# An audio tower on one core: the router's exponential takes the negated maximum as a bias, and every engine's steps are reordered

## The chip, the cores and the metric

The kernel runs on one core of a Trainium2 chip. The metric is the device time of one execution in microseconds. Of the kernel before, three runs are shown: 429.63, 430.35 and 431.35, median 430.35.

The core has five instruction queues that work side by side and wait for each other through semaphores: TensorE (PE in the rows, its weight loads PEld), VectorE (DVE), ScalarE (ACT), GpSimd (POOL) and SyncE (SP), which here starts all DMA transfers.

## The reference

The input x holds 16 sequences of 375 rows of 128 numbers. Each goes through three stages, the last two added to their input:

```
z, f, o = tanh / sigmoid / sigmoid of a width-2 convolution of x     # 374 rows
c_t = f_t c_(t-1) + (1 - f_t) z_t;   h = o * c                       # recurrence
a  = layernorm(h)
q, k, v = a W_qkv + b;  scores over 39 offsets back (0..32, 48, 64, 96, 128, 192, 256)
h  = h + (softmax(scores) v * if_gain * sigmoid(a W_gate + b)) W_out + b_out
x2 = layernorm(h)
logits = x2 router_w                                                  # 64 experts
probs  = softmax(logits), the two largest; an expert takes its first 128 tokens
y  = gelu(x2 w1 + b1) w2 + b2
h  = h + y * (sum of the kept probabilities of the token)
```

All experts share w1 and w2, so a token needs only the sum of its kept probabilities. The order of arrival at an expert runs over all 16 sequences, so the room that is left is carried from one sequence to the next.

## The kernel before

**Tiling.** A sequence is one unit of work: 374 columns in tiles of 128 partitions (channels), or three tiles of 128 tokens (TT = 3) where tokens lie on the partitions. Big buffers come in pairs, by the parity of the sequence. Eight PSUM banks of 512 columns are shared by name: the table HOME says which bank each intermediate result (z, f, o, k, q, v, g, logits "lg", positions "pos", up0 to up3, down "dn" and so on) has, and two names with one bank must follow each other.

**A sequence's way.** The convolutions (L405, L406), tanh on ACT (L808 to L819) and the scan on VectorE give h. Norm 1: statistics on VectorE (L1220, L1224), then ACT's logarithm, exponential and rows (L830, L835, L841), turned by TensorE and copied back (L854). TensorE projects k, q and the gate (L424, L432) and the values (L440). The attention's products of q with k at each offset come from VectorE (`products`, L1247, five a sequence) and POOL (`local_products`, L1724, three of about 3 us; `far_products`, L1709, seven shorter ones); TensorE sums them per head (`score`, L456), ACT copies the scores (L883), TensorE turns them to tokens (`turn_scores`, L468), VectorE adds the bias and does the maximum (L1266 to L1275), ACT the exponentials. The 33 nearest offsets become a band matrix: SP writes the weights to DRAM with a skewed stride (`write_attn`, L277) and reads them back as a band (`read_band`, L283); TensorE turns it (`turn_band`, L477) and multiplies it by the values (`attend`, L489). The six far offsets are handled elementwise on VectorE (`near_values`, L1294) and POOL (`far_values`, `far_sum`). Sum, norm, gate (L1304, L1312, L1320), out projection (L505) and residual (L1327) follow, then norm 2.

**The router.** TensorE gives the logits, tokens on partitions, 64 experts wide (`logits`, L521). ACT copies them to SBUF (`logit_copy`, L956); VectorE finds each tile's eight largest (`route_max`, L1352); POOL subtracts the largest from all logits (`router_subtract`, L1761, semaphore lsub_ready), and ACT takes the exponential and its sum per token (`router_exp`, L965). In between VectorE overwrites all but the two largest of the eight (L1360), replaces these two in a copy of the logits (`route_picks`, L1364) and so gets the mask (`route_mask`, L1372). TensorE counts positions from it (L539 to L543), VectorE compares them with the room left (`keep`, L1379), POOL multiplies mask and probability (`kept_mask` L1766, `kept_weights` L1772). Beside it run up projection (L529), gelu (L972) and down projection (L552). `finish` (L1410) and `store_out` end the sequence.

**What sets the order.** Nothing plans at run time. Each engine's code has a function `turn(at)` that issues one turn of a software pipeline: at(4), for instance, is the sequence that entered the pipeline four turns earlier. A list before the loop issues the first sequences' steps, `pipeline(engine, turn, range)` repeats the turn, and a list behind it issues the last sequences' steps. Each queue runs strictly in that order; a step that waits holds up all behind it on its engine. In TensorE's steps, the names in brackets are the results that had the bank before and must have been read. `after(engine, semaphore, n)` waits for a buffer's last reader.

Of the kernel before, what the change touches and what calls it, by code (L numbers as in the profile page):

```python
# [77 lines left out]
def build(nc, x, params, out):  # L78
# [5 lines left out]
    with ExitStack() as ctx:  # L84
# [12 lines left out]
        def P(name, a=0, b=None):  # L97
            lo, hi = COL[name]
            if lo >= PCOLS:
# [58 lines left out]
        HOME = dict(z=4, f=1, o=7, ht=2, xb=0, q=3, k=7, v=1, g=5, s0=4, s2=5, s1=5, ts0=4, ts1=3, ts2=5, tb0=1,  # L158
                    tb1=0, tb2=6, pv=1, ot=1, op=0, x2b=4, lg=6, pos=7, up0=0, up1=5, up2=7, up3=4, dn=6)
# [43 lines left out]
        msk_ready, pos_mm, lsub_ready = sem("msk_ready"), sem("pos_mm"), sem("lsub_ready")  # L203
# [55 lines left out]
        def _(sp):  # L259
# [78 lines left out]
            def turn(at):  # L338
                a0, a3, a4, a6 = at(0), at(3), at(4), at(6)
                if a4:  # L340
                    read_far(a4)
                if a0 and not (isinstance(a0.b, int) and a0.b < 3):
                    load_x(a0)
                if a4:
                    write_attn(a4)
                    read_values(a4)
                    read_band(a4)
                if a3:
                    write_values(a3)
                    read_near(a3)  # L350
                if a6:
                    store_out(a6)

            load_x(seq[3])
            write_values(seq[0])
            load_x(seq[4])
            read_near(seq[0])
            read_far(seq[0])
            write_attn(seq[0])
            read_values(seq[0])  # L360
            read_band(seq[0])
            write_values(seq[1])
            read_near(seq[1])
            pipeline(sp, turn, range(5, 17))
            read_far(seq[13])
            write_attn(seq[13])
            read_values(seq[13])
            write_values(seq[14])
            read_band(seq[13])
            read_near(seq[14])  # L370
            read_far(seq[14])
            write_attn(seq[14])
            read_values(seq[14])
            read_band(seq[14])
            write_values(seq[15])
            read_near(seq[15])
            read_far(seq[15])
            store_out(seq[11])
            write_attn(seq[15])
            read_values(seq[15])  # L380
# [10 lines left out]
        def _(pe):  # L391
# [164 lines left out]
            def turn(at):  # L556
                a0, a1, a2, a3, a4, a5, a6, a7 = at(0), at(1), at(2), at(3), at(4), at(5), at(6), at(7)
                if a4:
                    score(a4, 2, 0, ("s1", a4), first=True)
                    score(a4, 0, 3, last=True)  # L560
                    score(a4, 2, 1, last=True)
                if a3:
                    turn_x(a3, ("op", a6), ("up0", a7), ("tb1", a6), ("xb", a4))
                if a4:
                    turn_scores(a4, 1, ("q", a4))
                    turn_scores(a4, 0, ("s0", a4))
                    turn_scores(a4, 2, ("s2", a4))
                if a5:
                    turn_band(a5, 0, ("f", a1), ("v", a4), ("ot", a6), head=True)
                    turn_band(a5, 2, ("dn", a7), ("lg", a7), ("tb2", a6))  # L570
                if a3:
                    project(a3, "k", ("pos", a7), ("up2", a7), ("o", a2), head=True)
                    project(a3, "q", ("ts1", a4), ("q", a4))
                if a5:
                    turn_band(a5, 1, ("xb", a3), ("op", a6))
                if a6:
                    turn_x2(a6, ("ts0", a4), ("s0", a4), ("z", a1), ("up3", a7))
                if a5:
                    attend(a5, 0, ("tb0", a5), head=True)
                    attend(a5, 2)  # L580
                    attend(a5, 1)
                if a1:
                    convolve(a1, 2, ("k", a3), ("pos", a7), ("up2", a7), ("o", a2))
                if a6:
                    up(a6, 3, ("x2b", a6), head=True)
                    logits(a6, ("tb2", a5), ("dn", a7))
                if a5:
                    turn_o(a5, ("pv", a5))
                if a6:
                    up(a6, 0, ("tb1", a5), ("xb", a3), ("op", a6))  # L590
                if a0:
                    convolve(a0, 0, ("up3", a6), ("x2b", a6), ("ts0", a4), ("s0", a4), ("z", a1), head=True)
                if a6:
                    up(a6, 2, ("o", a1), ("k", a3), ("pos", a7))
                    up(a6, 1, ("ts2", a4), ("s2", a4), ("s1", a4), ("g", a4), ("up1", a7))
                if a5:
                    out_project(a5, ("up0", a6), ("tb1", a5))
                if a3:
                    value_project(a3, ("ot", a5), ("pv", a5), ("tb0", a5), ("f", a1))
                    project(a3, "g", ("up1", a6), ("ts2", a4), ("s2", a4), ("s1", a4), ("g", a4))  # L600
# [1351 lines left out]
```

## Time and profile before

| what | value |
|---|---|
| median of three runs | 430.35 us |
| span of the profiled execution | 428.5 us |
| busy: PE, VectorE, POOL, ACT | 405.3, 380.8, 372.7, 323.1 us |
| DMA, mean of 16 engines | 131 GB/s |
| bytes moved | 56.08 MB |
| granted TensorE clock | 1.00 in every repeated turn |

The profile records the span, from first to last instruction; 430.35 − 428.5 = 1.85 us lie between it and the runs' median.

To read the span, find something that recurs. The first instruction of a line that occurs once a sequence comes every 24.54 us in the middle of the span: that is the pipeline's turn. The stretch from 93.79 on holds ten turns, up to 337.03. Ahead of it the pipeline fills, behind it it drains, with the stretch behind 379.97 the emptiest: there TensorE is busy for 37.27 of 48.53 us, VectorE for 32.15, POOL for 23.37.

A row of a timeline gives an instruction's start and length, or a run of like instructions (x2, x3) as one row from the first's start to the last's end. Rows of one engine overlap a little: an instruction's start is recorded before the end of the one ahead of it. In brackets stands the time in which the engine stood idle before, and what ended it.

### The profile page before, as it was taken

The numbers are of one execution on the slowest core, as the hardware profiler recorded it, in microseconds if no ns is written. First come the engines' busy times: TensorE is split into PE (matmuls) and PEld (weight loads), VectorE is DVE, ScalarE is ACT, GpSimd is POOL, SyncE is SP. The second block draws the span as 40 slices with busy tenths as digits, with TensorE's granted clock in tenths as the row PEclk, the third lists the DMA queues.
The fourth block names the chain that finished last, engine by engine and source line by source line (L and its number), as shares of the span: only waits on it lengthen the run. The fifth ranks groups of instructions, "written<-read, shape, count | busy, mean of one in ns | idle before, by whom it ended". The sixth has DMA issues, their size and how long they took to land.

```text
span 428.5 us, 12683 instructions
## 1 busy us (share of the span) xinstructions
PE 405.3 (95%) x4554; PEld 278.6 (65%) x4554; DVE 380.8 (89%) x873; ACT 323.1 (75%) x728; POOL 372.7 (87%) x391
## 2 busy tenths in 40 slices
PE   8788789999999999999999999999999999998884
PEld 5444364776757676776767677676767675766763
DVE  2586999899999999999999999999999999999563
ACT  3756768879687877968687887868788796859773
POOL 7696999999989989898998989898998999997611
PEclk9999999999999999999999999999999999999998
DMA  6530866462737265372826446273735547265500
GB/s 230 192 105 2 200 165 182 105 174 62 200 88 183 79 154 150 86 207 61 198 71 149 143 120 186 55 201 82 178 95 129 158 109 190 65 182 127 133 13 24
DMA packets 78702, 56.08 MB, mean 131 GB/s; under 512 B 28304, under 2 KB 71344, under 8 KB 78512
## 3 DMA queue, kind: packets, MB, share of 16 engines
q1 hardware_dynamic: 78640, 55.28, 48.1%
q8 instruction: 36, 0.59, 0.6%
q14 instruction: 26, 0.21, 0.2%
HBM read 35.56 MB, written 19.70 MB: 129 GB/s over the span
## 4 chain that ended last, share of the span: by engine, by line
PE 74%; POOL 8%; issue 3%; DVE 3%; DMA 2%; ACT 1%; SPq 0%; POOLq 0%; DVEq 0%; ACTq 0%
PE bank L456 18%; PE bank L552 9%; PE bank L529 8%; PE bank L432 6%; PE bank L405 5%; PE bank L489 5%; PE bank L406 5%; PE bank L477 4%; POOL prod L1724 4%; POOL fprod L1709 3%; PE bank L468 3%; PE bank L521 2%; PE bank L505 2%; PE bank L440 2%; PE bank L424 1%
## 5 line engine op out<-in xcount | busy, mean ns | idle before, releaser
L1724 POOL TENSOR_TENSOR prod<-q,k 128x1448 f32<-128x1448 f32 (+2 forms) x48 | 145.6, 3053 | 17.4 <-ACT k L865 13.0
L1247 DVE SCALAR_TENSOR_TENSOR prod<-bank,par,k 128x1432 f32<-128x1432 f32 (+4 forms) x80 | 134.9, 1693 | 0.0
L456 PE MATMUL bank<-prod,ew 128*32 128x374 f32 (+7 forms) x1024 | 84.3, 467 | 2.4 <-ACT gate L872 1.0
L1709 POOL TENSOR_TENSOR fprod<-q,k 128x326 f32<-128x326 f32 (+6 forms) x112 | 79.0, 742 | 0.0
L456 PEld LDWEIGHTS bank<-prod,ew 128*32 128x32 f32 x1024 | 31.4, 110 | 44.9 <-issue 37.9
L972 ACT ACTIVATE hid<-bank,par 128x374 f32<-128x374 f32 x64 | 36.3, 575 | 23.8 <-PE bank L529 22.0
L799 ACT ACT_TABLE_LOAD x40 | 51.3, 1283 | 1.4 <-PEq L1944 0.7
L529 PE MATMUL bank<-x,par 128*128 128x374 f32 x128 | 48.4, 484 | 2.0 <-ACT x L925 2.0
L552 PE MATMUL bank<-par,hid 128*128 128x128 f32 x384 | 47.9, 276 | 0.0
L552 PEld LDWEIGHTS bank<-par,hid 128*128 128x128 f32 x384 | 45.9, 192 | 2.5
L405 PE MATMUL bank<-xT,par 128*128 128x374 f32 x96 | 40.9, 508 | 1.2 <-DVE mixin L1200 0.6
L432 PE MATMUL bank<-xn,par 128*128 128x374 f32 x96 | 35.8, 482 | 4.3 <-DVE near L1294 2.5
L883 ACT ACTIVATE scT<-bank 128x374 f32<-128x374 f32 (+2 forms) x48 | 21.7, 470 | 23.1 <-PE bank L456 22.9
L406 PE MATMUL bank<-xT,par 128*128 128x374 f32 x96 | 38.0, 477 | 0.0
L1756 POOL TENSOR_TENSOR near<-near 128x384 f32<-128x384 f32 x32 | 32.4, 1013 | 1.6 <-DVE near L1294 1.6
L1756 POOL TENSOR_TENSOR near<-near,far 128x256 f32<-128x256 f32 (+1 forms) x48 | 30.9, 643 | 2.4
L529 PEld LDWEIGHTS bank<-x,par 128*128 128x128 f32 x128 | 22.4, 190 | 12.7 <-ACT x L925 2.4
L901 ACT ACTIVATE bandT<-bank 128x512 f32<-128x512 f32 (+1 forms) x48 | 26.2, 584 | 5.5 <-PE bank L477 5.5
L406 PEld LDWEIGHTS bank<-xT,par 128*128 128x128 f32 x96 | 18.4, 191 | 12.1 <-issue 0.3
L489 PE MATMUL bank<-v,bandT 128*32 128x32 f32 x1536 | 26.1, 239 | 0.0
L477 PE MATMUL bank<-par,band 128*128 128x128 f32 (+1 forms) x192 | 25.6, 270 | 0.3 <-DMA band<-band_scratch 0.3
L489 PEld LDWEIGHTS bank<-v,bandT 128*32 128x32 f32 x1536 | 23.5, 127 | 2.9 <-issue 2.8
(123 smaller groups left out, 873.6 us busy)
## 6 DMA issues: line engine op xcount, KB each, us to landing
band<-band_scratch SPq DMA_DIRECT2D x16, 768.0 KB, 5.5
band_scratch<-attn SPq DMA_DIRECT2D x64, 180.4 KB, 3.0
vnear<-v_scratch SPq DMA_DIRECT2D x48, 192.0 KB, 3.1
v<-v_scratch SPq DMA_DIRECT2D x32, 192.0 KB, 4.1
v_scratch<-vtok SPq DMA_DIRECT2D x16, 192.0 KB, 3.0
xT<-x_dram SPq DMA_DIRECT2D x16, 187.5 KB, 3.4
vfar<-v_scratch SPq DMA_DIRECT2D x16, 128.0 KB, 3.3
out_dram<-osb SPq DMA_DIRECT2D x16, 128.0 KB
```

The costliest lines, as they stand in the source:

```text
L405: mm(dst, P("conv", 2 * g * D, (2 * g + 1) * D), xT[q_.s][:, 0:N], start=True, stop=False)
L406: mm(dst, P("conv", (2 * g + 1) * D, (2 * g + 2) * D), xT[q_.s][:, 1:N + 1], start=False, stop=True).then_inc((z_mm, f_mm, o_mm)[g], 1)
L432: mm(home(what)[:, 0:N], weights, xn[q_.s][:, 0:N], start=True, stop=True)\
L456: done = mm(home(f"s{c}")[32 * g:32 * g + 32, lo:N], ew[:, COLS[c] + j, :], src[:, j, lo:N], start=first or only, stop=last or only)
L489: done = mm(home("pv")[BT * u:BT * (u + 1), t * D + i:(t + 1) * D:PAIRS], bandT[t][:, i * 128 + u * BT:i * 128 + (u + 1) * BT], pair, star ...
L529: mm(home(f"up{f}")[:, 0:N], P("up", f * 128, (f + 1) * 128), x2[:, 0:N], start=True, stop=True)\
L552: done = mm(home("dn")[:, t * D:(t + 1) * D], hid[:, f, t * 128:(t + 1) * 128], P("down", f * D, (f + 1) * D), start=(f == 0), stop=(f == ...
L799: act.preload_act_table_set(name)
L1247: v.scalar_tensor_tensor(bass.AP(prod[c][:, :, :].tensor, first * N + lo, [[CW * N, 128], [N, w], [1, N - lo]]), home("q")[:, lo:N].unsque ...
L1709: last = g.tensor_tensor(fprod[:, i, o:N], q[q_.s][:, o:N], k[q_.s][:, KPAD:KPAD + N - o], ALU.mult)
L1724: g.tensor_tensor(bass.AP(prod[c][:, :, :].tensor, first * N + lo, [[CW * N, 128], [N, w], [1, N - lo]]), q[q_.s][:, lo:N].unsqueeze(1).br ...
L1756: g.tensor_tensor(near[:, 0, t0:TT, :], near[:, 0, t0:TT, :], term, ALU.add).then_inc(acc_added[i], 1)
```

## The change

In the router, `router_exp` reads the logits themselves and takes the negated maximum as its bias, one column per tile of tokens. VectorE computes these columns, `least`, with one instruction at the head of `route_picks`; POOL's `router_subtract` and the buffer lsub are gone, and the waits on lsub_ready move to exr_ready (the end of the exponentials) or least_ready. Ten names of HOME get another bank, and the bracketed names in TensorE's steps follow from them. The start lists, the turns and the end lists of all five engines are written in another order. The rest of the arithmetic is as it was.

```
-        lsub, exr = (sb(n, [128, TT, EXPERTS]) for n in ("lsub", "exr"))
+        exr = sb("exr", [128, TT, EXPERTS])
+        least = sb("least", [128, TT])
...
-        HOME = dict(z=4, f=1, o=7, ht=2, xb=0, q=3, k=7, v=1, g=5, s0=4, s2=5, s1=5, ts0=4, ts1=3, ts2=5, tb0=1,
-                    tb1=0, tb2=6, pv=1, ot=1, op=0, x2b=4, lg=6, pos=7, up0=0, up1=5, up2=7, up3=4, dn=6)
+        HOME = dict(z=4, f=6, o=7, ht=2, xb=0, q=3, k=0, v=1, g=5, s0=4, s2=5, s1=5, ts0=4, ts1=1, ts2=5, tb0=3,
+                    tb1=0, tb2=4, pv=1, ot=1, op=0, x2b=6, lg=6, pos=1, up0=0, up1=7, up2=4, up3=4, dn=7)
...
             def turn(at):                                  # TensorE
-                    convolve(a0, 1, ("v", a3), ("ot", a5), ("pv", a5), ("tb0", a5), ("f", a1))
+                    convolve(a1, 1, ("lg", a7), ("f", a2))
...
             def logit_copy(q_):
                 act.wait_ge(logit_mm, q_.b + 1)
                 after(act, msk_ready, q_.b)
-                after(act, lsub_ready, q_.b)
+                after(act, exr_ready, q_.b)
...
             def router_exp(q_):
                 table(LOG)
-                act.wait_ge(lsub_ready, q_.b + 1)
+                act.wait_ge(least_ready, q_.b + 1)
...
-                    done = A(exr[:, t, :], lsub[:, t, :], ACT.Exp, accum_out=smr[:, t:t + 1])
+                    done = A(exr[:, t, :], lg[:, t, 0:EXPERTS], ACT.Exp, bias=least[:, t:t + 1], accum_out=smr[:, t:t + 1])
...
             def turn(at):                                  # ACT
+                if a3:
+                    norm1_rows(a3)
                 if a4:
+                    score_copy(a4, 0)
                     score_copy(a4, 2)
...
+                if a6:
+                    norm2_rows(a6)
+                if a3:
+                    copy_k(a3)
...
             def route_max(q_):
                 dve.wait_ge(lg_ready, q_.b + 1)
-                after(dve, lsub_ready, q_.b)
...
             def route_picks(q_):
                 dve.wait_ge(m8_ready, q_.b + 1)
+                after(dve, exr_ready, q_.b)
+                v.tensor_scalar(least[:, :], m8[:, :, 0], -1.0, None, ALU.mult).then_inc(least_ready, 1)
                 v.memset(m8[:, :, TOPK:8], ABOVE).then_inc(top_ready, 1)
...
-            def router_subtract(q_):
-                pool.wait_ge(m8_ready, q_.b + 1)
-                after(pool, exr_ready, q_.b)
-                g.tensor_tensor(lsub[:, :, :], lg[:, :, 0:EXPERTS], m8[:, :, 0:1].broadcast_to([128, TT, EXPERTS]),
-                                ALU.subtract).then_inc(lsub_ready, 1)
...
             local_products(seq[15], 2)                     # POOL, the end list
-            router_subtract(seq[12])
+            far_products(seq[15], 0)
             kept_mask(seq[12])
-            far_products(seq[15], 0)
+            far_products(seq[15], 1)
             kept_weights(seq[12])
-            far_products(seq[15], 1)
...
             load_x(seq[3])                                 # SP, the start list
-            write_values(seq[0])
-            load_x(seq[4])
-            read_near(seq[0])
```

Three places show what moved. In such a listing a row is a line, an operation, and result<-operands with their shapes. Lines behind L139 have other numbers in the changed kernel.

ACT, the start, from the gate of sequence 0 on: the norm of sequence 1 is the rows rstd, rstd, xrow and xn1, scT is a copy of scores of sequence 0 (from bank 5 or 4), k1 and q1 are the projections of sequence 1. Before:

```order
L872 ACTIVATE gate0<-bank5,hbias 128x374
L799 ACT_TABLE_LOAD
L830 ACTIVATE rstd<-bank2,eps16 128x3
L883 ACTIVATE scT<-bank5 128x374
L835 ACTIVATE rstd<-rstd 128x3
L841 ACTIVATE xrow<-bank2,shift,rstd 128x128 x3
L854 ACTIVATE xn1<-bank0 128x374
L883 ACTIVATE scT<-bank4 128x358
L883 ACTIVATE scT<-bank5 128x342
L865 ACTIVATE k1<-bank7,par 128x374
L859 ACTIVATE q1<-bank3,par 128x374
L891 ACTIVATE vtok1<-bank1 128x384
```

and now:

```order
L817 ACT_TABLE_LOAD
L848 ACTIVATE rstd<-bank2,eps16 128x3
L853 ACTIVATE rstd<-rstd 128x3
L859 ACTIVATE xrow<-bank2,shift,rstd 128x128 x3
L866 ACTIVATE hkeep1<-bank2 128x384
L901 ACTIVATE scT<-bank5 128x374
L909 ACTIVATE vtok0<-bank1 128x384
L872 ACTIVATE xn1<-bank0 128x374
L901 ACTIVATE scT<-bank4 128x358
L883 ACTIVATE k1<-bank0,par 128x374
L877 ACTIVATE q1<-bank3,par 128x374
L901 ACTIVATE scT<-bank5 128x342
```

The logarithm, the exponential and the rows of the norm (rstd, rstd, xrow) now stand together ahead of the first copy of scores, which was between them; vtok0, the values of sequence 0, comes behind that copy; k1 and q1 stand ahead of the third copy instead of behind it.

VectorE, a repeated turn, just behind the first product of a sequence, up to the router's mask and the residual. prod is the second product, the rows with near and onorm belong to the attention of other sequences, h<-bank,cell is the recurrence's output, ao the gate, m the router's eight largest, msk its mask, h<-bank,hkeep the residual. Before:

```order
L1304 TENSOR_TENSOR bank<-bank,near 128x384
L1312 TENSOR_TENSOR onorm<-bank,rs 128x384
L1294 TENSOR_TENSOR near<-bank,vnear 128x1152
L1214 SCALAR_TENSOR_TENSOR h<-bank,cell 128x374
L1320 SCALAR_TENSOR_TENSOR ao<-bank,par,gate 128x374
L1352 MAX m<-lg 128x8 x3
L1247 SCALAR_TENSOR_TENSOR prod<-bank,par,k 128x1496
L1360 MEMSET m 128x3x6
L1364 MATCH_REPLACE bank<-m,lg 128x70 x3
L1372 TENSOR_TENSOR msk<-bank,lg 128x192
L1327 TENSOR_TENSOR h<-bank,hkeep 128x384
```

and now:

```order
L1327 TENSOR_TENSOR bank<-bank,near 128x384
L1335 TENSOR_TENSOR onorm<-bank,rs 128x384
L1317 TENSOR_TENSOR near<-bank,vnear 128x1152
L1343 SCALAR_TENSOR_TENSOR ao<-bank,par,gate 128x374
L1374 MAX m<-lg 128x8 x3
L1237 SCALAR_TENSOR_TENSOR h<-bank,cell 128x374
L1383 TENSOR_SCALAR least<-m 128x3
L1384 MEMSET m 128x3x6
L1388 MATCH_REPLACE bank<-m,lg 128x70 x3
L1270 SCALAR_TENSOR_TENSOR prod<-bank,par,k 128x1496
L1350 TENSOR_TENSOR h<-bank,hkeep 128x384
L1396 TENSOR_TENSOR msk<-bank,lg 128x192
```

The picks (MEMSET, MATCH_REPLACE), with least ahead of them, stand before the second product and no longer behind it; the residual stands ahead of the mask, the gate and the maximum ahead of the recurrence's output.

POOL, the end: the last local product (128x4x366) and the far products (fprod) of sequence 15, with the router of sequence 12 among them (lsub its subtraction, kept the mask, kw the weights). Before:

```order
L1724 TENSOR_TENSOR prod<-q,k 128x4x366
L1761 TENSOR_TENSOR lsub<-lg,m 128x192
L1766 TENSOR_TENSOR kept<-kept,msk 128x192
L1709 TENSOR_TENSOR fprod<-q,k 128x326
L1709 TENSOR_TENSOR fprod<-q,k 128x310
L1709 TENSOR_TENSOR fprod<-q,k 128x278
L1709 TENSOR_TENSOR fprod<-q,k 128x342
L1772 TENSOR_TENSOR kw<-kept,exr 128x192
L1709 TENSOR_TENSOR fprod<-q,k 128x246
L1709 TENSOR_TENSOR fprod<-q,k 128x182
L1709 TENSOR_TENSOR fprod<-q,k 128x118
L1756 TENSOR_TENSOR near<-near 128x384
```

and now:

```order
L1756 TENSOR_TENSOR prod<-q,k 128x4x366
L1741 TENSOR_TENSOR fprod<-q,k 128x326
L1741 TENSOR_TENSOR fprod<-q,k 128x310
L1741 TENSOR_TENSOR fprod<-q,k 128x278
L1741 TENSOR_TENSOR fprod<-q,k 128x342
L1793 TENSOR_TENSOR kept<-kept,msk 128x192
L1741 TENSOR_TENSOR fprod<-q,k 128x246
L1741 TENSOR_TENSOR fprod<-q,k 128x182
L1741 TENSOR_TENSOR fprod<-q,k 128x118
L1799 TENSOR_TENSOR kw<-kept,exr 128x192
L1788 TENSOR_TENSOR near<-near 128x384
```

The subtraction is gone, the mask has moved behind four of the far products and the weights behind all seven.

## Rows read from the trace of the kernel before

**Rows 1.** The page's busy line: busy us (share of the span) xinstructions, by engine.

```profile
PE 405.3 (95%) x4554; PEld 278.6 (65%) x4554; DVE 380.8 (89%) x873; ACT 323.1 (75%) x728; POOL 372.7 (87%) x391
```

**Rows 2.** Busy time of each engine in three stretches, from:to length.

```profile
93.79:118.33 24.54, 24.54 (x286) 17.32 (x285) 23.46 (x55) 19.40 (x46) 24.07 (x26) 1.00 0.52 138
...
314.65:337.03 22.38, 22.18 (x277) 15.72 (x277) 22.10 (x49) 18.25 (x43) 21.16 (x21) 1.00 0.52 138
...
359.00:379.97 20.97, 20.96 (x270) 14.66 (x269) 20.32 (x50) 16.62 (x40) 20.73 (x21) 1.00 0.51 129
```

**Rows 3.** POOL's timeline, end of sequence 15: start, length, operation, [idle before].

```profile
379.10 0.52 POOL L1761 TENSOR_TENSOR lsub<-lg,m 128x192 f32<-128x192 f32 x1
...
383.35 0.60 POOL L1772 TENSOR_TENSOR kw<-kept,exr 128x192 f32<-128x192 f32 x1
```

**Rows 4.** ACT by line and shape: busy us, mean ns | idle before.

```profile
L872 ACT ACTIVATE gate<-bank,hbias 128x374 f32<-128x374 f32 x16 | 9.2, 574 | 0.4 <-PE bank L432 0.4
...
L854 ACT ACTIVATE xn<-bank 128x374 f32<-128x374 f32 x16 | 7.7, 484 | 1.0 <-PE bank L424 1.0
```

**Rows 5.** VectorE's timeline, a repeated turn (153 to 162) and the end.

```profile
153.28 1.70 DVE L1247 SCALAR_TENSOR_TENSOR prod<-bank,par,k 128x1432 f32<-128x1432 f32 x1
...
158.75 1.76 DVE L1247 SCALAR_TENSOR_TENSOR prod<-bank,par,k 128x1496 f32<-128x1496 f32 x1
160.46 0.07 DVE L1360 MEMSET m<- 128x18 f32 x1
...
161.30 0.36 DVE L1372 TENSOR_TENSOR msk<-bank,lg 128x192 bf16<-128x192 f32 x1
161.60 0.56 DVE L1327 TENSOR_TENSOR h<-bank,hkeep 128x384 f32<-128x384 f32 x1
...
407.39 0.48 DVE L1352 MAX8 m<-lg 128x8 f32<-128x64 f32 x3
...
408.66 0.60 DVE L1320 SCALAR_TENSOR_TENSOR ao<-bank,par,gate 128x374 f32<-128x374 f32 x1
```

**Rows 6.** VectorE's timeline, the setup.

```profile
4.23 1.24 DVE L1187 TENSOR_SCALAR hbias<-par 128x12 f32<-128x12 f32 x1 [3.28 <-DMA par<-params_dram]
...
16.22 0.83 DVE L1193 CAST onesb<-par 128x128 bf16<-128x128 f32 x1
16.97 0.84 DVE L1194 TENSOR_SCALAR outg<-par 128x128 f32<-128x128 f32 x1
```

**Rows 7.** POOL's timeline, the setup; the two later rows are windows of one group.

```profile
4.06 1.38 POOL L1668 MEMSET v<- 128x1536 f32 x1
...
15.43 1.53 POOL L1693 TENSOR_TENSOR bm<-prod 128x312 f32<-128x312 f32 x2
...
15.43 2.29 POOL L1693 TENSOR_TENSOR bm<-prod 128x312 f32<-128x312 f32 x3
```

**Rows 8.** TensorE's timeline, a repeated turn (152 to 163) and the end.

```profile
152.24 0.60 PE L477 MATMUL bank<-par,band 128*128 128x128 f32 x4
...
162.70 0.19 PE L540 MATMUL bank<-msk,beforeb 128*128 128x64 bf16 x1
...
411.32 0.19 PE L540 MATMUL bank<-msk,beforeb 128*128 128x64 bf16 x1 [1.01 <-DVE msk L1372]
```

**Rows 9.** POOL's timeline, the start (39.44) and a repeated turn.

```profile
39.44 9.06 POOL L1724 TENSOR_TENSOR prod<-q,k 128x1448 f32<-128x1448 f32 x3 [3.50 <-ACT k L865]
...
153.15 6.08 POOL L1724 TENSOR_TENSOR prod<-q,k 128x1448 f32<-128x1448 f32 x2 [1.07 <-ACT k L865]
159.17 0.53 POOL L1761 TENSOR_TENSOR lsub<-lg,m 128x192 f32<-128x192 f32 x1
```

**Rows 10.** ACT's timeline at the start: the copy of sequence 0's first scores.

```profile
32.03 0.48 ACT L883 ACTIVATE scT<-bank 128x374 f32<-128x374 f32 x1 [2.02 <-PE bank L456]
```

**Rows 11.** The chain of waits near the end: start, length, what.

```profile
402.49 1.47 PE bank L477 x12
403.97 0.63 PE bank L529 x2
```

More of the change, by code:

```diff
@@ new lines, in turn @@
+                if a4:
+                    project(a4, "g", ("ts2", a5))
+                if a1:
+                    convolve(a1, 1, ("lg", a7), ("f", a2))
+                if a7:
+                    down(a7, 0, ("up1", a7), head=True)
+                    down(a7, 1)
+                    positions(a7, ("v", a4))
+                if a3:
+                    turn_h(a3, ("ht", a4))
+                if a7:
+                    down(a7, 2)
+                if a4:
+                    score(a4, 1, 0, ("g", a4), first=True)
+                    score(a4, 1, 1)
+                    score(a4, 0, 1, ("z", a1), ("up2", a7), first=True)
+                    score(a4, 1, 3)
+                    score(a4, 1, 2, last=True)
+                    score(a4, 0, 0)
+                    score(a4, 0, 2)
@@ L699, in _ @@
+            turn_h(seq[15], ("ht", seq[14]))
+            down(seq[11], 0, ("up1", seq[11]), head=True)
+            positions(seq[11], ("v", seq[14]))
+            score(seq[14], 1, 2, last=True)
+            score(seq[14], 0, 1, ("up2", seq[11]), first=True)
+            down(seq[11], 1)
+            down(seq[11], 2)
+            score(seq[14], 0, 0)
+            score(seq[14], 0, 2)
+            score(seq[14], 0, 3, last=True)
             score(seq[14], 2, 0, ("s1", seq[14]), first=True)
-            score(seq[14], 0, 3, last=True)
@@ new lines, in turn @@
+                if a6:
+                    attention_gate(a6)
+                if a7:
+                    route_max(a7)
+                if a2:
+                    recur_out(a2)
+                if a7:
+                    route_picks(a7)
+                if a4:
+                    products(a4, 1, 0)
+                if a6:
+                    residual(a6)
+                if a7:
+                    route_mask(a7)
+                if a4:
+                    products(a4, 0, 2)
+                    products(a4, 0, 0)
@@ new lines, in turn @@
+                if a1:
+                    recur_in(a1)
+                if a7:
+                    keep(a7)
+                if a6:
+                    stats2(a6)
+                if a7:
+                    add_b2(a7)
+                if a3:
+                    stats1(a3)
+                if a6:
+                    shift2_rows(a6)
+                if a4:
+                    products(a4, 0, 3)
+                if a7:
+                    take_room(a7)
+                if a3:
+                    shift_rows(a3)
@@ L1580, in _ @@
             route_max(seq[12])
+            products(seq[15], 1, 0)
             route_picks(seq[12])
```

869 lines of the change are left out of this document (439 added, 430 removed).

## The prediction

> **What bounds the kernel now.** I read the busy line first, then the span cut into turns, then the queues of the engines at the start, in a repeated turn and at the end. The busy line [rows 1] puts TensorE at 95%, VectorE at 89% and POOL at 87%. The table of turns [rows 2] tells more. From 93.79 us on, the same turn comes back ten times, 24.54 us each: (337.03 − 93.79 − 22.38) / 9 = 24.54 for nine of them, and a tenth of 22.38 that has no more convolutions to start. In such a turn TensorE is busy for all 24.54 us; VectorE for 23.46. POOL's 24.07 in the first of them holds work left over from the start. So the middle costs what TensorE's work costs: no order can shorten it by much, but a late operand lengthens it. The last turn shown has 20.96 of 20.97 us on TensorE and 20.73 on POOL, so there POOL and VectorE have nothing to spare. What an order can win lies before 93.79 and after 379.97.
>
> **The subtraction and what replaces it.** POOL loses sixteen subtractions of 0.52 us [rows 3], 8.3 us of work. In the ten repeated turns that is worth nothing, since TensorE sets the turn. Near the end it counts: before the last far products of sequence 15 POOL now has neither the subtraction (0.52) nor kept_weights (0.60), which moved behind them [rows 3].
>
> ACT's three exponentials now read a bias column. No row shows them in that form, but ACT rows of one shape do with and without a column: 574 against 484 ns [rows 4], 90 ns more. Three are 0.27 us a turn; ACT has over 5 us a turn free by [rows 2] (19.40 busy of 24.54), so it costs only on the final chain: +0.3.
>
> VectorE gets one new instruction, least = −max, 128x3, read from and written to SBUF, in front of route_picks' memset. By the memset's row it would take 0.07 us [rows 5] and I would take 0.1. But no row of a repeated turn shows a single-source VectorE operation of this kind. The setup does, and there it looks different [rows 6, 7]: hbias, 128x12, lasts 1.24 us, from 4.23 to 5.47, where POOL's memset ends at 5.44; the cast of onesb ends at 17.05, POOL's second table add at 16.96; outg ends at 17.81, POOL's third at 17.72. Three times of three, the operation ends 0.03 to 0.09 us after the POOL instruction that was running. So least may last until POOL's current instruction ends: anything from 0 to a whole product, 3.05 us.
>
> The Trainium skill (SBUF — State Buffer, Who interferes with whom) says that a VectorE tensor_scalar or cast from SBUF to SBUF can take both port pairs, one of which POOL shares under an exclusive lock, and that whoever comes second waits the whole instruction out; a page beside it (VectorE: DVE Perf Modes, Mode 2×_2P) admits an odd outermost count when source and destination match, as the 3 here does. By that rule the wait is there in each turn; a 0.1 us instruction would instead give the first rival below. The three setup rows agree with it.
>
> How long in a repeated turn? [rows 8] and [rows 9] place it. POOL's first two products start at 153.15, 0.91 us after the q projection's end at 152.24, and end at 159.17 by the start of the next POOL instruction (6.02 us, though the row's own length is 6.08). VectorE starts its first product at 153.28 and its second at 158.75 [rows 5]: 5.47 us for the product, attention sum and norm, near values, recur_out, gate and maximum. In the new order exactly these stand between that product and least, so least is issued at about 158.75 on that clock and is held until 159.17 plus 0.09: 0.5 us. Bounds: 0, and 3.05 if it falls just behind a product's start. I take 0.5.
>
> Who waits for it? VectorE goes on with the picks (160.46 to 161.30, 0.84), the product (160.46 − 158.75 = 1.71), the residual (0.56, less the 0.06 by which such rows overlap: 161.30 + 0.36 against 161.60) and the mask (0.36) [rows 5]. So the mask ends 0.5 + 0.1 + 0.84 + 1.71 + 0.5 + 0.36 = 4.0 us after 158.75, or 9.6 after POOL's start. The f convolution of the newest sequence now shares bank 6 with the logits and must wait for this mask. TensorE's work between the q projection's end and that convolution is the same set that stands in the old turn between 152.24 and 162.70 [rows 8]: 10.46 us. POOL starts 0.91 us into it now; norm2's three rows, which ACT now does ahead of copy_k and copy_q, add some 0.4 (an estimate: 1.16 us of ACT, part of it beside TensorE's own lead). The mask is thus wanted 9.15 us after POOL's start and comes at 9.6: TensorE idles about 0.4 us a turn. Without the hold it comes at 9.1, just in time. Ten turns: **+4.0 us** (bounds 0 and, at a whole product each, over 20).
>
> In the last three turns VectorE works without a break, so a hold there moves the end directly. A random moment meets half a product, 1.5 us; 0.5 of it falls into what those turns leave free (0.3 by VectorE's 22.10 of 22.38, 0.65 by 20.32 of 20.97 [rows 2]). Three times 1.0: **+3.0** (bounds 0 and 9).
>
> **The start.** The norm of sequence 1 waits in ACT's queue behind a copy of scores: the queue stands 2.02 us until scores arrive at 32.03, and only then come the exponential and the rows [rows 10]. Now logarithm, exponential and rows stand together ahead of that copy, and k and q no longer stand behind the third copy. POOL waits 3.50 us for k of sequence 1 before its products at 39.44 [rows 9]; I expect that wait nearly gone, up to 3.1 us earlier. On VectorE the statistics of that norm move back behind two more products, and at the start SP's load of x for sequence 4 stands behind the writing of the values of sequence 0, so its convolution comes later, with the work behind it. VectorE's last product of sequence 2 then becomes what TensorE waits for, and it gains less than POOL. Ends: 0 and −3.1; I take **−1.9**.
>
> **The end.** After sequence 15's weights have gone through DRAM, the chain runs through TensorE and VectorE. One up projection of sequence 14 (0.63 us) stands in it between the band and the attention [rows 11]; it is now done before. VectorE does the maximum and picks of sequence 14 between norm and gate of sequence 15, from 407.39 to 408.66 [rows 5]; now the gate comes first, minus what turn_o takes, −0.8. TensorE's down projections of sequence 14 stood behind positions, which waited 1.01 us for a mask [rows 8]; now they come first: −0.6. The last logits share no bank with the down results any more: −0.5. Against that, softmax_far now runs ahead of softmax_dense, and the sum of sequence 14 ahead of sequence 15's scores: +0.6. Together **−1.9**, with the bias columns −1.6. Ends: 0, if each finds another wait behind it, and −3.5, were nothing given back.
>
> **Sum.** −1.9 + 4.0 + 3.0 − 1.6 = +3.5 us on the profiled 428.5. The runs' median is 430.35, 1.85 above that span, which I keep: 430.35 + 3.5 = **433.8**. Its own range: 430 to 440.
>
> **The rivals.**
> First, on the other side: no hold, because three elements with a stride behave otherwise than the setup's operations, or because it falls where something else waits. Then −1.9 − 1.6 = −3.5, and the many tight hand-overs of the new turn (mask to convolution, norm to turn_o, norm2 behind the band copy) may give back 0 to 1: about 427.0. For it: no row of a repeated turn shows the hold. Against: three rows of three.
> Second, the hold falls just after a product's start and lasts 3 us: VectorE's turn is then 23.46 + 3.0 = 26.5 us, 2 above TensorE's, and with the tail 430.35 − 3.5 + 20 + 9 = about 455. It decides when VectorE comes 0.42 us later than I place it (159.17 − 158.75). Against: gate and maximum wait for TensorE's turn_o and logits, which pins VectorE to the turn.
> Third, the subtraction was worth its whole 8.3 us, because POOL paces the kernel: 422. Against: in the turns POOL too stands waiting for k, 1.07 us at 153.15 [rows 9].
>
> **How the numbers follow.** Forecast 0.57, first rival 0.33, second 0.05, third 0.05. A change under 0.5% (2.2 us) can't be told from none here, so the borders are 428.2 and 432.5. Slower: 0.44 of the forecast and the second rival, 0.49. Within: 0.10 and 0.10 of the first two, 0.20. Faster: the rest of the first, the third and 0.03: 0.31. The range takes in the forecast's own and most of the first rival: 425 to 441.
>
> **What would show it.** The row of least on VectorE: 0.1 us or several times that, its end on POOL's; TensorE's waits for the mask in every turn; the turn's length, 24.54 or about 24.9; POOL's wait for k of sequence 1; the time from the last band product of sequence 15's weights to the end, 428.5 − 402.49 = 26.0 us before [rows 11]. I am wrong if least is short, or if it is long and TensorE does not wait.

## The result, and the profile after

The changed kernel takes 436.79 us (median of five runs) against 430.35. One of the five took 446.05 us and is left out of the ratio, which is 1.0133, with a 95% interval of 1.0098 to 1.0167. A second set of runs, on another occasion, gave 435.31 against 429.96: 1.0123 (1.0109 to 1.0138). So it is 1.2 to 1.3% slower, 5 to 6 us, where 3.5 were forecast.

The second set's profile is the one to compare with [rows 1]. Its span is 434.2 us, 5.7 more than before. Its busy line, as in [rows 1]:

```profile
PE 410.1 (94%) x4554; PEld 280.2 (65%) x4554; DVE 391.8 (90%) x889; ACT 324.6 (75%) x728; POOL 364.9 (84%) x375
```

VectorE's new row is 16 instructions; a row by line groups them (durations in ns, minimum, median, maximum):

```profile
L1383 DVE TENSOR_SCALAR least<-m x16: 168/490/1978, 80.3 to 422.1; 128x3 f32<-128x3 f32 x16
```

Half a microsecond for three numbers a partition. A repeated turn, POOL's row first, then VectorE's from least to the mask, then TensorE's weight load for the f convolution, which waits for that mask, and the convolution's products. The last row is the window of a turn: from:to, length, busy time of TensorE, its weight loads, VectorE, ACT and POOL, granted clock, DMA share, GB/s.

```profile
149.92 9.06 POOL L1756 TENSOR_TENSOR prod<-q,k 128x1448 f32<-128x1448 f32 x3 [2.22 <-issue]
...
155.52 0.48 DVE L1383 TENSOR_SCALAR least<-m 128x3 f32<-128x3 f32 x1
155.95 0.07 DVE L1384 MEMSET m<- 128x18 f32 x1
...
156.68 1.77 DVE L1270 SCALAR_TENSOR_TENSOR prod<-bank,par,k 128x1496 f32<-128x1496 f32 x1
158.36 0.55 DVE L1350 TENSOR_TENSOR h<-bank,hkeep 128x384 f32<-128x384 f32 x1
158.82 0.35 DVE L1396 TENSOR_TENSOR msk<-bank,lg 128x192 bf16<-128x192 f32 x1
...
159.22 0.30 PEld L415 LDWEIGHTS bank<-xT,par 128*128 128x128 f32 x2 [0.38 <-DVE msk L1396]
...
159.28 0.84 PE L415 MATMUL bank<-xT,par 128*128 128x374 f32 x2
...
180.14:204.77 24.63, 24.63 (x286) 17.21 (x285) 23.98 (x57) 19.49 (x47) 21.89 (x22) 1.00 0.48 132
```

least is issued 5.60 us behind POOL's first product (155.52 − 149.92) and ends at 156.00. POOL's three products take 9.06 / 3 = 3.02 us each, so the second ends at 149.92 + 2 × 3.02 = 155.96: least lasts until then. The weight load, which runs ahead of its matmuls, waits 0.38 us for the mask; the matmuls have no wait of their own. The turn is 24.63 us against 24.54 [rows 2].

To see where the 5.7 us lie, cut the span at milestones that each order has: ACT's copy of x2 (L925, L943 after) of sequences 0, 1 and 10, then the start of VectorE's score subtraction of sequence 15 (L1275, L1298 after), then the end. Each number is a difference of two row starts, and each row one execution: the changed kernel's took 435.95 us, e2's 434.01, e5's 435.99, e9's 437.25, e10's 428.94, e12's 428.62.

| profile | to x2 of 0 | 0 to 1 | 1 to 10 | 10 to scores of 15 | scores of 15 to end | span |
|---|---|---|---|---|---|---|
| before | 79.48 | 24.83 | 220.86 | 64.03 | 39.30 | 428.5 |
| changed | 75.17 | 25.98 | 222.59 | 67.41 | 43.05 | 434.2 |
| e2, held all the same | 77.12 | 24.62 | 222.60 | 67.42 | 40.44 | 432.2 |
| e5, no hold | 78.27 | 24.57 | 221.16 | 66.47 | 43.73 | 434.2 |
| e9, values early | 80.13 | 25.14 | 222.60 | 67.42 | 40.21 | 435.5 |
| e10, both | 78.39 | 24.58 | 221.16 | 63.42 | 39.55 | 427.1 |
| e12, both, least on VectorE | 76.45 | 24.57 | 221.16 | 65.77 | 38.85 | 426.8 |

In the changed kernel's row the start gained 4.3, the turn behind it lost 1.15, the middle lost 1.7, and 7.1 us were lost behind sequence 10: 3.4 in the last turns, 3.75 after them. The middle and the last turns come out alike in e2, which is held in the same way; start and end differ from one execution to the next.

The first profile, of a 446.05 us execution, differs from this one chiefly in one place: the first of the sixteen holds. VectorE's and POOL's rows there, and TensorE's convolution behind it:

```profile
81.52 9.66 DVE L1383 TENSOR_SCALAR least<-m 128x3 f32<-128x3 f32 x1
...
80.25 6.10 POOL L1756 TENSOR_TENSOR prod<-q,k 128x1480 f32<-128x1480 f32 x2
86.28 4.87 POOL L1741 TENSOR_TENSOR fprod<-q,k 128x326 f32<-128x326 f32 x7
...
94.40 1.61 PE L415 MATMUL bank<-xT,par 128*128 128x374 f32 x2 [8.96 <-DVE msk L1396]
```

There least came 1.27 us into a product and got its turn only when POOL had nothing ready any more, nine instructions later (two products, seven far products, to 91.15). The other fifteen lasted 0.17 to 1.99 us, to the end of POOL's running instruction where there was one; none of the six other profiles with a held least shows one like the first, and why POOL kept its turn here is open.

### The profile page after: what moved, and what is told of

Its sections match the earlier page's. It is cut to its first block and busy times, and to the rows that moved or that the text cites. A ratio compares the mean times of both kernels' runs of the same rounds, so it can differ in the third digit from the quotient of the medians.

```text
span 444.3 us, 12667 instructions
## 1 busy us (share of the span) xinstructions
PE 412.4 (93%) x4554; PEld 281.8 (63%) x4554; DVE 399.5 (90%) x889; ACT 324.8 (73%) x728; POOL 365.0 (82%) x375
## 5 line engine op out<-in xcount | busy, mean ns | idle before, releaser
L466 PE MATMUL bank<-prod,ew 128*32 128x358 f32 (+7 forms) x1024 | 84.2, 468 | 1.8 <-DVE mixin L1223 1.1
L539 PE MATMUL bank<-x,par 128*128 128x374 f32 x128 | 51.7, 508 | 1.5 <-ACT x L943 1.3
L562 PEld LDWEIGHTS bank<-par,hid 128*128 128x128 f32 x384 | 47.0, 195 | 5.8 <-issue 1.7
L562 PE MATMUL bank<-par,hid 128*128 128x128 f32 x384 | 49.0, 279 | 0.7 <-ACT hid L990 0.5
L442 PE MATMUL bank<-xn,par 128*128 128x374 f32 x96 | 38.2, 485 | 0.9 <-DVE near L1317 0.7
L1793 POOL TENSOR_TENSOR kept<-kept,msk 128x192 f32<-128x192 f32 x16 | 8.8, 553 | 28.4 <-DVE kept L1403 28.3
L919 ACT ACTIVATE bandT<-bank 128x512 f32<-128x512 f32 (+1 forms) x48 | 27.7, 586 | 5.0 <-PE bank L487 5.0
L415 PEld LDWEIGHTS bank<-xT,par 128*128 128x128 f32 x96 | 16.4, 195 | 21.6 <-DVE msk L1396 14.0
L487 PE MATMUL bank<-par,band 128*128 128x128 f32 (+1 forms) x192 | 28.8, 279 | 0.0
```

The lines of the kernel that those rows point to most:

```text
L415: mm(dst, P("conv", 2 * g * D, (2 * g + 1) * D), xT[q_.s][:, 0:N], start=True, stop=False)
L442: mm(home(what)[:, 0:N], weights, xn[q_.s][:, 0:N], start=True, stop=True)\
L466: done = mm(home(f"s{c}")[32 * g:32 * g + 32, lo:N], ew[:, COLS[c] + j, :], src[:, j, lo:N], start=first or only, stop=last or only)
L487: done = tr(home(f"tb{t}")[:, i * 128:i * 128 + n], band[0:n, t, i * 128:(i + 1) * 128], ident[0:n, 0:n])
L539: mm(home(f"up{f}")[:, 0:N], P("up", f * 128, (f + 1) * 128), x2[:, 0:N], start=True, stop=True)\
L562: done = mm(home("dn")[:, t * D:(t + 1) * D], hid[:, f, t * 128:(t + 1) * 128], P("down", f * D, (f + 1) * D), start=(f == 0), stop=(f == ...
```

## The experiments

Two theories stood at first. The hold theory: least's wait for POOL costs the time. The order theory: the new order itself does, above all at the end. Ratios are to the kernel before in the same set of runs.

**e1, the changed kernel again**, for a second profile.

> The changed kernel unchanged, for a second profile: in the first one the first of the sixteen holds of least lasted 9.66 us (81.52 to 91.18, through the end of nine POOL instructions) and all others ended with the POOL instruction that was running. Theory A (the long hold is a rare event of that execution): here every hold ends with the running POOL instruction, 0.4 to 2 us each, and the span is 9 us shorter, 433 to 436. Theory B (the start's order brings it about each time): a hold of some 9 us at the first sequence again. Time 434 to 438 under both, since four of the five runs were there.

435.31 us. The first hold is 1.84 us, from 1.26 us into the same product to that product's end: theory A, the long hold is rare.

**e2, another form of least.**

```
-  v.tensor_scalar(least, m8[:, :, 0], -1.0, None, ALU.mult)
+  v.scalar_tensor_tensor(least, m8[:, :, 0], -2.0, m8[:, :, 0], ALU.mult, ALU.add)
```

> The changed kernel, but least computed as -2m + m with VectorE's scalar_tensor_tensor, the form whose 128x3 rows (shift) last 0.15 us in every turn beside POOL. Hold theory: least lasts about 0.15 us each time; the steady turns go from 24.63 to 24.54 (-0.9 in ten), the holds of the last three turns go (1.40 + 0.77 + 1.99 = -4.2) and one slip of 1.0: 429 to 432, no execution near 446. Order theory (the new order's own hand-overs cost the time, the hold is covered): 435 to 437, and the loss stays in the turns behind sequence 9.

434.30 us, 1.0116 (1.0092 to 1.0141), between the two theories. The edit did not take the hold away: the other form is held just as long, as its row shows (the last one under e12 is the contrast).

```profile
L1383 DVE SCALAR_TENSOR_TENSOR least<-m x16: 164/486/1980, 82.2 to 421.6; 128x3 f32<-128x3 f32 x16
```

**e3, the new order with POOL's subtraction** in the turn's second gap between local products, no least.

```
-  after(dve, exr_ready, q_.b); v.tensor_scalar(least, ...)
+  router_subtract(a11)          # POOL, between local_products(a8, 1) and (a8, 2)
```

> The changed order and banks, but with POOL's subtraction as before (between the second and third local product of a turn) and no least, no bias column. Hold theory: as without the hold, 429 to 432, plus up to 1 us where POOL's 0.52 us stand in the last turns. Order theory: 435 to 438.

432.86 us, 1.0059 (1.0042 to 1.0076), runs from 429.9 to 434.0. Better than the changed kernel by 2.4 us, and still slower than before: the hold is part of the loss, not all of it. Its last turns take 67.51 us, with the late values that e9 is about.

**e4, the old order with VectorE's least**, at the head of the picks.

> The order and banks of before; only the router's arithmetic is changed: least with the two-operand-free tensor_scalar at the head of the picks, behind the second product, no subtraction on POOL. Hold theory: the picks start 160.46 in a turn whose third POOL product then starts at 159.17 and ends at 162.2, so least lasts 1.8 us a turn; VectorE's turn becomes 23.46 + 1.8 = 25.3 against TensorE's 24.54, and the positions wait for the mask: ten turns cost 7 to 17 us, 437 to 447. Order theory (the hold costs nothing): 429 to 431.

443.71 us, 1.0332 (1.0311 to 1.0354). One turn, VectorE's and POOL's rows, and the turn's window:

```profile
162.64 1.80 DVE L1361 TENSOR_SCALAR least<-m 128x3 f32<-128x3 f32 x1
...
155.36 9.05 POOL L1726 TENSOR_TENSOR prod<-q,k 128x1448 f32<-128x1448 f32 x3 [0.80 <-ACT k L866]
...
144.22:169.58 25.36, 24.70 (x287) 17.25 (x286) 25.05 (x56) 19.77 (x46) 21.94 (x21) 1.00 0.55 144
```

1.80 us was forecast and came; the row ends at 164.44, POOL's third product at 164.41. VectorE is now busy for 25.05 us of a turn of 25.36 (23.46 in [rows 2]). This is the hold in the old order (e6 has the same arithmetic without it): where it falls 1.3 us into a product, it costs 13.7 us.

**e5, no hold in the new order**: ACT makes the columns (0.19 us) from the maximum.

```
 def router_exp(q_):
+    A(least, m8[:, :, 0], ACT.Copy, scale=-1.0).then_inc(least_ready, 1)
 def route_picks(q_):
-    v.tensor_scalar(least, m8[:, :, 0], -1.0, None, ALU.mult).then_inc(least_ready, 1)
```

> The changed kernel, but the bias columns come from ACT (a copy of the maximum with scale -1 ahead of the three exponentials, some 0.2 us): neither VectorE's least nor POOL's subtraction is left, so no hold anywhere. Hold theory (the holds of the last three turns, 1.40 + 0.78 + 1.98 us, delay the end by their length, those of the middle by 0.06 a turn): the second profile's 434.2 us of span less 4.2 and 1, 430 to 431 by the clock of the runs. Tail theory (most of the loss lies behind sequence 15's scores, where ACT's and TensorE's new order makes TensorE wait and its granted clock falls): 432.5 to 434, with the copy of sequence 15's second norm about 3.5 us later than before's 414.87.

433.76 us, 1.0088 (1.0056 to 1.0119), runs from 431.0 to 436.0. The middle is 221.16 us, as it should be without a hold, but the last turns take 66.47 all the same, and the end 43.73. Two of the seven runs, 431.0 and 431.3, lie where the hold theory put them or just above; the profiled one, of 435.99, does not. So the hold theory as it stood falls: something stands behind the hold.

**e6, the old order with the same arithmetic as e5.**

> The order and banks of before with the same arithmetic as the last one: POOL's sixteen subtractions gone, the negated maximum as a bias column made by ACT. This is the change without its order and without VectorE's instruction. The forecast's view (the subtraction is worth nothing in the turns, a little at the end): 429 to 430.5. If POOL's time paced the kernel: 422 to 426.

430.18 us, 1.0007 (0.9998 to 1.0015). POOL's 8 us of subtractions were worth nothing.

**e7, pieces of the old end**: band and attention of sequence 15 ahead of up projection and logits of 14 (TensorE), far exponential and band copies early (ACT), sum and norm ahead of the maximum (VectorE).

> The changed kernel with three pieces of its end list written as before had them: TensorE turns and attends sequence 15's band ahead of the up projection and logits of sequence 14, ACT takes sequence 15's far exponential behind its dense one and copies the band ahead of gelu, VectorE does sum and norm of sequence 15 ahead of the maximum and picks of sequence 14. Tail theory: the span falls by 2 to 3.5 us, to 432 or 433 by the runs. Hold theory: the end is moved by the holds alone, so this changes less than 1 us: 434.5 to 436.

433.82 us, 1.0094 (1.0079 to 1.0108) where the changed kernel had 1.0123: between the two theories. The last stretch is 40.27, at a granted clock of 0.95.

**e8, extra matrix products in two gaps of the end.**

```
+  warm(4, ("tb0", seq[14]))     # four unread products 128x374
   turn_x2(seq[14], ("lg", seq[13]))
+  warm(2)
   ... and 3 + 2 around turn_x2(seq[15])
```

> The changed kernel with eleven matrix products more, whose results nobody reads, in two gaps of the end where TensorE waits for sequence 14's and 15's second norm (4 + 2 and 3 + 2 of 128x374). In the second profile the granted clock falls to 0.50 behind the first gap (403.8 to 409.0) and to 0.59 in the last up projections (421.0 to 424.4). Clock theory: it stays at 1.00 there, which gives back 2.6 and 1.4 us less what the extra products are in the way (0.3 to 0.6): 431.5 to 433. If the clock is not the cost, or the gaps not its cause: 435 to 436.

435.79 us, 1.0138 (1.0124 to 1.0152): no gain, but the clock is at 1.00. The changed kernel's rows (TensorE's two waits, the band of sequence 15, two windows whose third column from the right is the granted clock), then e8's first filling products and its windows:

```profile
402.60 0.51 PE L523 MATMUL bank<-par,xrow 128*128 128x128 f32 x3 [1.17 <-ACT xrow L936]
403.78 1.59 PE L539 MATMUL bank<-x,par 128*128 128x374 f32 x2 [0.66 <-ACT x L943]
...
406.33 2.70 PE L487 MATMUL bank<-par,band 128*128 128x128 f32 x12
...
403.78:406.33 2.55, 2.55 (x8) 1.98 (x9) 2.11 (x7) 1.73 (x2) 2.47 (x4) 0.50 0.11 31
...
421.00:424.40 3.40, 3.40 (x10) 1.91 (x11) 1.73 (x12) 1.57 (x4) 0.00 (x0) 0.59 0.21 56
```

```profile
403.56 2.76 PE L521 MATMUL bank<-xT,par 128*128 128x374 f32 x8
...
403.78:413.00 9.22, 9.22 (x135) 6.77 (x134) 5.83 (x24) 5.32 (x11) 5.95 (x9) 1.00 0.28 96
...
421.00:424.40 3.40, 3.40 (x16) 2.38 (x15) 1.51 (x9) 2.88 (x5) 0.00 (x0) 1.00 0.19 51
```

A granted clock of 0.50 is the lower of the two levels (1.2 GHz of 2.4): the band's 12 products take 2.70 us against 1.47 in [rows 11]. With the extra products the clock stays up, but the first four of them (two records each, so eight in the row) take 2.76 us where the wait that they fill was 1.17; what the clock gives back, they take. In its profile the end is 41.5 us against 43.05, and the start 77.8 against 75.17. So this run does not settle what the clock alone costs.

**e9, values early**: one step of SP's end list.

```
   read_band(seq[12])
+  read_values(seq[12])
   store_out(seq[9])
   read_near(seq[13])
-  read_values(seq[12])
```

> The changed kernel with one step of SP's end list moved: the values of sequence 12 are read from DRAM ahead of the store of sequence 9 and of the near values of sequence 13, not behind both. In the profiles of the changed order TensorE stands before the attention of sequence 12 with no engine that it waits for, 1.22 us with the hold (347.87) and 2.64 us without it, while these two reads, issued from 341.1 on, land. Transfer theory: that wait goes, 434 to 434.5, since the holds of 1.40 and 0.78 us around it stay. If the wait is not the transfer's: 435 to 436, with the wait where it was.

435.31 us, 1.0101 (1.0069 to 1.0132). No change beyond the noise, where 434 to 434.5 was expected. TensorE's wait before the attention of sequence 12 is gone; the last turns still take 67.42, and TensorE waits there for the mask of sequences 10 and 12:

```profile
338.83 0.19 PE L550 MATMUL bank<-msk,beforeb 128*128 128x64 bf16 x1 [1.03 <-DVE msk L1396]
...
384.70 0.19 PE L550 MATMUL bank<-msk,beforeb 128*128 128x64 bf16 x1 [1.28 <-DVE msk L1396]
```

**e10, no hold and values early.**

> ACT makes the bias columns (no hold) and SP reads the values of sequence 12 early. Transfer theory (the transfer stands behind the hold and took over what its removal gave): 433.8 less 2.6, 431 to 431.5. If hold and transfer add nothing to each other: 433 to 434.

428.31 us, 0.9954 (0.9939 to 0.9970): 7 us better than the changed kernel and faster than the kernel before. What e5 and e9 failed to give apart, they give together, and more: 431 at the least was expected. Of the 7.1 us between the two profiles 4.0 lie in the last turns, as the transfer theory has it; 3.5 lie in the end stretch, where it named nothing (see the end, below). The attention of sequence 12 on TensorE in the changed kernel, e5 and e10:

```profile
347.87 1.65 PE L499 MATMUL bank<-v,bandT 128*32 128x32 f32 x96 [1.22 <-issue]
```

```profile
348.39 1.64 PE L499 MATMUL bank<-v,bandT 128*32 128x32 f32 x96 [2.64 <-issue]
```

```profile
345.83 1.96 PE L499 MATMUL bank<-v,bandT 128*32 128x32 f32 x96
```

SP's issue of these values in the changed kernel and in e10 (the second of the two reads lands at 347.78 in the changed kernel and at 348.30 in e5, 0.09 us before the products that use it):

```profile
341.07 1.57 SPq L301 DMA_DIRECT2D v<-v_scratch  x2
```

```profile
337.24 1.54 SPq L301 DMA_DIRECT2D v<-v_scratch  x2
```

Last, the windows of the last turns, from x2 of sequence 10 to the scores of 15, in the changed kernel, e9 and e10 (busy TensorE, its weight loads, VectorE, ACT, POOL):

```profile
323.74:391.15 67.41, 63.66 (x797) 43.55 (x792) 65.57 (x145) 50.41 (x118) 62.50 (x60) 1.00 0.59 143
```

```profile
327.87:395.29 67.42, 64.04 (x798) 43.52 (x790) 66.38 (x145) 50.29 (x118) 62.47 (x60) 1.00 0.60 143
```

```profile
324.13:387.55 63.42, 63.12 (x797) 43.75 (x790) 61.82 (x142) 51.10 (x121) 62.10 (x60) 1.00 0.61 148
```

TensorE needs some 63.1 to 64 us here, VectorE 61.8. With the holds of these turns (1.40 + 1.69 + 1.98 = 5.1 us in e9) VectorE stands at 66.38 of 67.42 and is what the turns wait for, by way of the mask. Without them (e5), TensorE waits 2.64 us for the values instead. In these profiles either delay alone fills the stretch to 66.5 or 67.4.

**e11, e10 with the end of before** in more places (those of e7; sequence 15's far values read ahead of the band's writing, mask and positions of sequence 13 ahead of its down projection).

> As the last one, with the end as before had it: band and attention of sequence 15 ahead of sequence 14's up projection and logits on TensorE, far exponential early and band copies ahead of gelu on ACT, sum and norm of sequence 15 ahead of sequence 14's maximum on VectorE, far values of sequence 15 read ahead of the band's writing on SP, mask and positions of sequence 13 ahead of its down projection. If start, hold, transfer and end are all that the new order differs in: the start's gain of 2 stays and the rest goes, 427.5 to 429.5. If the end list isn't the cause: as the last one, 431.

429.72 us, 0.9988 (0.9967 to 1.0008): nothing gained over e10. Without hold and late values, the order of the end list is no cost of its own.

**e12, least from VectorE with one operand in PSUM, and values early.**

```
+  nought = home("lg")[:, 408:408 + TT]      # zeros, set once
-  v.tensor_scalar(least, m8[:, :, 0], -1.0, None, ALU.mult)
+  v.scalar_tensor_tensor(least, m8[:, :, 0], -1.0, nought, ALU.mult, ALU.add)
```

> The changed kernel with the values of sequence 12 read early and least still made by VectorE, but as -m + 0 with the zeros in three unused columns of the logits' PSUM bank (one memset of 128x3 at the first sequence more). Operand theory (an instruction of VectorE is held when all that it reads and writes lies in SBUF and it is of these two forms; with one operand in PSUM, as shift has, it isn't): least lasts about 0.15 us in every turn and the time is that of the version with ACT's copy, 428 to 428.8. If it is held all the same: 434 to 435.5, as with the early read alone.

428.78 us, 0.9958 (0.9943 to 0.9974).

```profile
L1388 DVE SCALAR_TENSOR_TENSOR least<-m,bank x16: 146/148/158, 81.7 to 416.3; 128x3 f32<-128x3 f32 x16
```

0.15 us, sixteen times of sixteen, with the operation and the shape of e2. The hold depends on where the operands lie. And VectorE may make the columns, so e10's gain was not ACT's doing. The last turns of this profile are 2.35 us longer than e10's, with one wait that e10 doesn't have, for the band:

```profile
342.61 0.63 PE L488 MATMUL bank<-par,band 128*128 128x128 f32 x4 [2.21 <-DMA band<-band_scratch]
```

Whether each execution has it is not known.

## Why the prediction was right, and where not

**The hold: right, to its size.** 0.5 us a turn was forecast, for an issue 158.75 − 153.15 = 5.60 us behind POOL's first product; 0.48 came, at 5.60 us. For the old order e4's expectation had 1.8, and 1.8 came. The Trainium skill (SBUF — State Buffer, Who interferes with whom) gives a second condition that the forecast did not use: an operation of VectorE with two inputs in SBUF meets POOL's reads on the shared port too. e2 and e12 agree, 0.49 against 0.15 us. The same section has the second comer wait for the whole instruction of the first; the other holds of the first profile agree, and the one of 9.66 us, past the ends of eight instructions, does not.

**The bias column: right.** 90 ns more for an exponential were forecast; it takes 332 ns against 240, by the medians.

**The subtraction: right.** e6: 1.0007.

**The start: right in the middle.** −1.9 was forecast. x2 of sequence 0 comes between 75.17 and 80.13 us in ten profiles of the new order (e1 to e3, e5, e7 to e12), median 77.75, against 79.48 in the median of three of the old one (before, e4, e6): −1.7. What spreads it by 5 us from one execution to the next is open; the profile compared above has the most, −4.3.

**The turns: mis-sized.** The term was +4.0, "TensorE idles about 0.4 us a turn". A turn is 24.63 us with the hold and 24.57 without it (e10: 221.16 / 9), so the hold costs 0.05 a turn. The step that failed is the distance between two moments. The mask was put 9.6 us behind POOL's start; it ended at 159.17 − 149.92 = 9.25. The forecast added least's own 0.1 us to the hold, which contains it, and from the picks to the mask it had 3.41 us where 3.22 came. And TensorE was put at 9.15; without a hold (e10) the convolution's products start 160.99 − 151.63 = 9.36 us behind POOL's start:

```profile
151.63 9.05 POOL L1758 TENSOR_TENSOR prod<-q,k 128x1448 f32<-128x1448 f32 x3 [1.96 <-issue]
...
160.99 0.79 PE L415 MATMUL bank<-xT,par 128*128 128x374 f32 x2
```

In the changed kernel they start at 9.36 too (159.28 − 149.92): the wait takes the weight load's lead, and the products, 0.84 us for 0.79, lose 0.05. Beside it one hold a run is longer: where POOL's end list begins, an addition of 0.99 us stands between its first two products, and least comes 1.65 us into a product instead of 2.63 (1.45 us, 1.0 lost). The middle is +1.7 and the turn ahead of it +1.15 in this profile, the latter from the first hold of 1.84; e2, whose first hold is 0.48, has 24.62 there, less than before.

**The last turns: right in size, short of a cause.** +3.0 was forecast for three holds of 1.5 us, 1.0 of each past the slack; 3.4 came, the holds there are 1.40, 0.78 and 1.98, and e9, without the late values, has 3.4 too. But the forecast had nothing on SP's queue: the values of sequence 12 now stand behind a store and the near values of sequence 13. That wait lies under the holds, and takes their place when they go (+2.4 in e5).

**The end: wrong in sign.** −1.9 + 0.3 was forecast from waits that the new list leaves out. It is 43.05 us against 39.30, and 39.55 in e10 with the same list: the list itself brings nothing (the bound 0 of that term), and the loss goes with the clock. This stretch before, in the changed kernel, in e2 and in e10:

```profile
389.20:428.50 39.30, 28.05 (x343) 21.71 (x332) 23.40 (x88) 26.74 (x61) 14.22 (x22) 0.97 0.29 70
```

```profile
391.15:434.20 43.05, 32.23 (x358) 25.02 (x348) 23.38 (x93) 27.07 (x59) 12.16 (x18) 0.84 0.22 58
```

```profile
391.76:432.20 40.44, 29.68 (x357) 23.14 (x346) 23.61 (x93) 26.82 (x59) 12.16 (x18) 0.91 0.23 62
```

```profile
387.55:427.10 39.55, 28.14 (x358) 21.82 (x348) 22.92 (x90) 27.24 (x62) 12.44 (x19) 0.98 0.28 69
```

TensorE's granted clock is 0.84 over it in the changed kernel and in e5, 0.97 before, 0.98 in e10. TensorE is busy 32.23 us in it against 28.05 before, for the same products: 4.2 us, more than the 3.75 lost. e2, held like the changed kernel, has a clock of 0.91 and 40.44 us: there the loss is 1.1. That the clock is the cause is argued from these pairs; the one test of it, e8, is undecided. Nor do the runs say why the clock fell there and not in e10, whose waits ahead of the same products are as long, 1.18 and 0.66 us, against 1.17 and 0.66:

```profile
399.23 0.52 PE L523 MATMUL bank<-par,xrow 128*128 128x128 f32 x3 [1.18 <-ACT xrow L936]
400.41 0.87 PE L539 MATMUL bank<-x,par 128*128 128x374 f32 x2 [0.66 <-ACT x L943]
```

e10 reaches the stretch without the stalls of the last turns, but that this decides was not shown.

**The rivals.** The first (no hold: 427.0) had its price nearly right and its condition wrong: without the hold alone the time is 433.8 (e5); 428.3 and 428.8 come when the late transfer goes as well. The whole-product rival came in no turn: the holds of the repeated turns are 0.5 us and once 1.45; e4 shows how dear another place in the product is. The POOL rival falls with e6.

The sum was nearer than its terms, which is luck: in this profile the turns were 2.3 too dear and the start gained 2.4 more than forecast, against an end 5.3 too cheap (−1.6 against +3.75) and 1.15 in the first turn.

## What to carry to other kernels

A small VectorE operation between two SBUF buffers can last until POOL's running instruction ends (up to 2.2 us here, once 9.66, for 0.15 us of work); give it one operand in PSUM, or to ACT, and place it by POOL's instruction ends if it must stay. When a suspected cost is removed and the time stays, look for what stands right behind it before giving up the theory: here each of two delays hid the other in the last turns (67.4 us, with one edit 66.5 or 67.4, with both 63.4), and only both edits together paid: 1.7% of the time, a good part of it by the clock at the end, where they had given 0.4% and, within the noise, 0.2%. In a queue that is written by hand, check each moved transfer against its reader: one read of values, three steps later in SP's list than before, cost the last turns 2.4 us where the holds alone cost 3.4.

## What was not expected

- A hold can outlast the instruction that it meets: 9.66 us over nine POOL instructions, once in the 112 of seven profiles, and TensorE waited 8.96 us behind it.
- `scalar_tensor_tensor` on 128x3 elements: 0.49 us (median) with both inputs in SBUF, 0.15 us with one in PSUM.
- Waits of 1.2 and 0.7 us on TensorE near the end went with more than 5 us at half the granted clock in two profiles (changed, e5) and with none in another (e10).
